# The row-maximum pass of self-attention multiplies 64 rows instead of 128

## Chip, cores and metric

The kernel runs on one core of one Trainium2 chip. The metric is device time in microseconds (us); lower is better.

## What is computed

One transformer block on `x` of shape (2, 1024, 256), with a 77-token context, and behind it a feed-forward layer with quantised weights. In float32:

```
h  = adaln(layernorm(x));  x1 = selfattention(h, h) @ wo + bo + x        # 16 heads of 64, 1024 keys
h2 = adaln(x1);            x2 = crossattention(h2, ctx) @ wo2 + bo2 + x1 # 77 keys
h3 = adaln(x2);            x3 = gated_ff(h3) + x2
out = x + x3 + bitlinear(gelu(bitlinear(layernorm(x + x3))))
scores = q @ k.T / sqrt(64);  attn = softmax(scores)                      # per head
```

Only the self-attention is touched by the change.

## The kernel before

All float32 products are made of float16 pairs: a high part and a low remainder, so that a product `w*x` is three products of float16 (`PASSES`). The work of attention is cut into 16 units of two heads each (`UNITS`; unit `g` holds heads of one batch). The operands of a head lie in `HB` (in the profile `head_operands`), 128 partitions by four fields of 1024 tokens: `QS` holds the high part of the queries in partitions 0 to 63 and the low part in 64 to 127; `KH` holds the high part of the keys in both halves. `QM` and `KL` hold the rest of what the score products need, with the negated row maximum in partition 64 of `QM`. These fields are filled by DMAs from `qk_pairs` (`restack`) and, for the maxima, from `neg_max_rows`.

Self-attention passes over the scores twice. The maximum pass (line 854) makes a 128 by 512 block of scores at a time: 8 tiles of 128 queries by 2 halves of 512 keys, for each of the two heads, so 32 products a unit and 512 in all. VectorE reduces each block to one maximum per query (line 1836, `maxes`), then the two halves to the negated maximum (line 1848), which TensorE transposes into rows (`row`, line 864; for the very first tiles line 867). The second pass makes the scores for the softmax (lines 898 and 899), ScalarE takes the exponential (line 1242), GpSimd or VectorE the float16 remainder (`exps_rest`, line 1568 or 1863), and TensorE multiplies by the values (lines 921 to 923), 48 small products a chunk.

The order on TensorE is written out by hand in `FIRST_UNIT` (unit 0) and `SELF_UNIT` (units 1 to 14); unit 15 takes its order from `unit()`. In it the maximum products of the next heads stand one, or two, at a time between pieces of scores, values, projections (`q`, `k`, `v`, lines 833 and 843; `proj`, line 810) and transposes (`out`, line 871; `norm_T`, line 796):

```
    ("max", 0, 1, 8), ("scores", 1), ("rest", 0), ("max", 0, 1, 9), ("q", 1, 0), ("max", 0, 1, 10), ("slot", 0),
    ("rest", 1), ("scores", 2), ("values", 0), ("rest", 2), ("q", 1, 1), ("scores", 3), ("max", 0, 1, 11),
```

Each maximum product goes to one of two banks of PSUM (`mixed`), and waits until VectorE has read what was in that bank. Setup work of unit 0 ("columns") transposes small arrays of 2 rows (line 765), 16 rows (line 785) and 77 rows (line 789) on TensorE.

Of the kernel before, what the change touches and what calls it, by code (L numbers as in the profile page):

```python
# [22 lines left out]
P = 128  # L23
B, S, D = 2, 1024, 256
CTX = 77
H, DH = 16, 64
# [7 lines left out]
HALF = 512  # L34
# [19 lines left out]
QS, QM, KH, KL = range(4)  # L54
# [354 lines left out]
def build(nc, x, cond, ctx_in, w, out):  # L409
# [6 lines left out]
    with es:  # L416
# [214 lines left out]
        def first_tile(ai, g, what):  # L631

            return TPH if (ai, g, what) == (0, 0, ("row", 0)) else 0
# [114 lines left out]
        def _(pe):  # L748
            mm, tr = nc.tensor.matmul, nc.tensor.transpose
# [3 lines left out]
            for k in range(KC):  # L753
                last = tr(M_[0][:, k * B:(k + 1) * B], condr[:, k * P:(k + 1) * P], identf[0:B, 0:B])
# [59 lines left out]
            def item(ai, g, what, m):  # L814

                a, s, kind = AT[ai], AT[ai].sem, what[0]
                b, hp, par = g // NP, g % NP, g % 2
                wc = [slice(hp * P + c * INNER, hp * P + c * INNER + P) for c in range(KC)]
                if kind in ("q", "k"):
                    if (ai, g) == (0, 0):  # L820
                        pe.wait_ge(hT_done, TPH * (what[1] + 1))
                        pe.wait_ge(split_done, 1 if kind == "q" else 2)
                    elif what == ("q", 0) and hp == 0:
                        pe.wait_ge(hT_done, NT * ai + TPB * (b + 1))
                        pe.wait_ge(split_done, 6 if ai else 2)
                    for n_, (wh, xh) in enumerate(PASSES):
                        for c in range(KC):
                            if kind == "q" or ai == 0:
                                o = b * S + what[1] * HALF
                                rhs = hT[:, xh, c, o:o + HALF]  # L830
                            else:
                                rhs = ctxT[:, xh, c, b, 0:CTX]
                            last = mm(m[:, 0:rhs.shape[-1]], W[:, 0 if kind == "q" else 1, wh, wc[c]], rhs,  # L833
                                      start=(n_ == 0 and c == 0), stop=(n_ == 2 and c == KC - 1))
                elif kind == "v":
                    if g == 0:
                        pe.wait_ge(split_done, 7 if ai else 3)
                    for i in range(a.v_tiles):
                        for n_, (wh, xh) in enumerate(PASSES):
                            for c in range(KC):  # L840
                                o = b * S + (what[1] * a.v_tiles + i) * P
                                lhs = hT[:, xh, c, o:o + P] if ai == 0 else ctxT[:, xh, c, b, 0:CTX]
                                last = mm(m[0:a.ks, i * P:(i + 1) * P], lhs, W[:, 2, wh, wc[c]],  # L843
                                          start=(n_ == 0 and c == 0), stop=(n_ == 2 and c == KC - 1))
                elif kind == "max":

                    _, h, t, kh = what
                    hb = HB[:, par, h, :, :]
                    if (t, kh) == (0, 0):
                        pe.wait_ge(s.heads[h], 16 * a.restack_dmas * (g + 1) + CREDIT)  # L850
                        if (ai, g) == (0, 0):
                            pe.wait_ge(cleared, 16)
                    if ai == 0:
                        last = mm(m[:, :], hb[:, QS, t * P:(t + 1) * P], hb[:, KH, kh * HALF:(kh + 1) * HALF],  # L854
                                  start=True, stop=True)
                    else:
                        for i in range(TPH):
                            q = t * TPH + i
                            last = mm(m[:, i * CTX:(i + 1) * CTX], hb[:, QS, q * P:(q + 1) * P], hb[:, KH, 0:CTX],
                                      start=True, stop=True)  # L860
                elif kind == "row":
                    pe.wait_ge(s.negmax, CREDIT + 2 * g + what[1] + 1)
                    t0 = first_tile(ai, g, what)
                    last = tr(m[0:TPB - t0, 0:P], nm[:, what[1], t0:TPB], identf[:, :])
                elif kind == "first":
                    pe.wait_ge(first_negmax, 1)
                    last = tr(m[0:TPH, 0:P], nm[:, 0, 0:TPH], identf[:, :])
                else:
                    pe.wait_ge(s.summed, CREDIT + 4 * g + 3 + what[1])
                    for i in range(TPH):  # L870
                        last = tr(m[:, i * P:(i + 1) * P], Osb[:, what[1] * TPH + i, :], identf[:, :])
                last.then_inc(s.item, 1)
# [54 lines left out]
            def piece(st):  # L927
                if st.after:
                    pe.wait_ge(*consumed(st.after))
                if st.kind == "item":  # L930
                    item(st.ai, st.g, st.what, ITEM[st.bank])
                elif st.kind == "proj":
                    project(st.ai, *st.what, st.g, st.bank)
                elif st.kind == "normT":
                    norm_T(st.g, st.bank)
                elif st.kind == "scores":
                    scores(st.ai, st.g, st.c)
                elif st.kind == "values":
                    values(st.ai, st.g, st.c)
                elif st.kind == "setup":  # L940
                    setup(st.what)
# [1261 lines left out]
```

## Time and profile before

| | |
|---|---|
| median of 2 runs | 1196.14 us (1196.13 to 1196.16) |
| the profiled execution, first to last instruction | 1200.9 us |
| TensorE (PE) busy | 1115.7 us (93%), 12740 products |
| VectorE (DVE) busy | 860.5 us (72%) |
| GpSimd (POOL) busy | 694.0 us (58%) |
| ScalarE (ACT) busy | 591.5 us (49%) |
| mean granted TensorE clock | 0.990 |

The page gives the profiled execution's span alone, 4.8 us (0.4%) above the median of the timed runs. A product's record on PE outlasts its slot, as products are pipelined, so slots are read from start to start. PEld is the load of the weights (the stationary operand), which has records of its own.

### The profile page before, as it was taken

What the parts mean: (1) busy time and instruction counts of PE and PEld (TensorE: products, weight loads), DVE (VectorE), ACT (ScalarE), POOL (GpSimd) and SP (SyncE); (2) the same over time, 40 slices, a digit from 0 to 9 for tenths busy, and PEclk for the clock granted to TensorE, in tenths of its full rate; (3) what the DMA queues carried; (4) which work ended last, traced back from release to release, by engine and by line L of the source; (5) the groups of instructions that cost most, each with busy time, mean ns of one, the idle gap of its engine ahead of it and who ended that gap; (6) DMA issues with size and microseconds to landing.
All of it is one profiled execution on the core that took longest, in us unless ns stands there. A gap on an engine that the chain in (4) does not pass through costs nothing.

```text
span 1200.9 us, 30653 instructions
## 1 busy us (share of the span) xinstructions
PE 1115.7 (93%) x12740; PEld 731.2 (61%) x12740; DVE 860.5 (72%) x1686; ACT 591.5 (49%) x856; POOL 694.0 (58%) x641
## 2 busy tenths in 40 slices
PE   4799999999999999999999999889899989999996
PEld 1355665665656656657656666567567766756664
DVE  6677767757657568677676576848878976786876
ACT  3445455444444444454443445544444544257677
POOL 5757866765655657777675656346535733533433
PEclk9899999999999999999999999999999989999999
DMA  8330220220220211202202203122433343000001
GB/s 286 86 92 1 55 54 2 55 54 3 54 54 2 55 28 28 55 5 52 54 2 54 54 2 89 41 54 60 136 77 74 72 128 124 1 1 9 15 14 36
DMA packets 41854, 63.52 MB, mean 53 GB/s; under 512 B 11459, under 2 KB 22383, under 8 KB 41461
## 3 DMA queue, kind: packets, MB, share of 16 engines
q1 hardware_dynamic: 40413, 60.91, 20.1%
q8 instruction: 101, 1.65, 0.6%
q10 hardware_dynamic: 1304, 0.66, 0.2%
q14 instruction: 36, 0.29, 0.1%
HBM read 20.63 MB, written 2.10 MB: 19 GB/s over the span
## 4 chain that ended last, share of the span: by engine, by line
PE 67%; DVE 15%; DMA 5%; ACT 5%; issue 4%; POOL 2%; SPq 1%; ACTq 0%; DVEq 0%
PE outs L833 9%; PE scores L898 7%; PE scores L899 7%; PE mixed L854 6%; PE outs L810 5%; PE scores L960 5%; PE outs L923 4%; PE outs L921 4%; DVE maxes L1836 4%; PE outs L922 4%; PE outs L974 4%; PE outs L843 3%; DVE exps_rest L1863 2%; DMA head_operands<-qk_pairs 2%; DMA head_operands<-neg_max_rows 2%
## 5 line engine op out<-in xcount | busy, mean ns | idle before, releaser
L1568 POOL TENSOR_TENSOR exps_rest<-exps 128x1024 f16<-128x1024 f32 (+1 forms) x297 | 510.4, 1723 | 308.3 <-ACT exps L1242 307.2
L1242 ACT ACTIVATE exps<-scores 128x1024 f32<-128x1024 f32 (+1 forms) x320 | 296.8, 937 | 262.9 <-PE scores L899 243.1
L1836 DVE TENSOR_REDUCE maxes<-mixed 128x1 f32<-128x512 f32 x512 | 334.8, 684 | 92.2 <-PE mixed L854 87.7
L921 PE MATMUL outs<-values,exps 128*128 128x65 f16 (+1 forms) x2176 | 227.2, 193 | 1.7 <-POOL exps_rest L1568 1.6
L922 PE MATMUL outs<-values,exps 128*128 128x64 f16 (+1 forms) x2176 | 227.2, 192 | 0.0
L923 PE MATMUL outs<-values,exps_rest 128*128 128x65 f16 (+1 forms) x2176 | 227.0, 194 | 0.0
L898 PE MATMUL scores<-head_operands 128*128 128x512 f16 (+1 forms) x576 | 218.6, 380 | 5.3 <-DMA head_operands<-neg_max_rows 4.7
L899 PE MATMUL scores<-head_operands 128*128 128x512 f16 (+1 forms) x576 | 218.5, 379 | 0.0
L921 PEld LDWEIGHTS outs<-values,exps 128*128 128x128 bf16 (+1 forms) x2176 | 201.9, 98 | 22.3 <-POOL exps_rest L1568 3.1
L922 PEld LDWEIGHTS outs<-values,exps 128*128 128x128 bf16 (+1 forms) x2176 | 200.9, 98 | 23.5
L923 PEld LDWEIGHTS outs<-values,exps_rest 128*128 128x128 f16 (+1 forms) x2176 | 200.8, 97 | 0.0
L854 PE MATMUL mixed<-head_operands 128*128 128x512 f16 x512 | 178.0, 384 | 18.2 <-DVE maxes L1836 9.8
L833 PE MATMUL outs<-hT,weights 128*128 128x512 f16 x492 | 123.8, 389 | 3.4 <-DVE qk_pairs L1821 2.4
L1821 DVE SCALAR_TENSOR_TENSOR qk_pairs<-outs,qk_pairs 128x512 f16<-128x512 f32 x82 | 56.4, 688 | 80.5 <-ACT qk_pairs L1207 80.5
L854 PEld LDWEIGHTS mixed<-head_operands 128*128 128x128 f16 x512 | 48.7, 97 | 78.0 <-DVE maxes L1836 34.7
L810 PE MATMUL outs<-weights,attn_outT 128*128 128x256 f16 x744 | 93.0, 276 | 0.0
L899 PEld LDWEIGHTS scores<-head_operands 128*128 128x128 f16 (+1 forms) x576 | 57.6, 100 | 48.9
L960 PE MATMUL scores<-hT,weights 128*128 128x512 f16 x384 | 86.8, 379 | 0.0
L898 PEld LDWEIGHTS scores<-head_operands 128*128 128x128 f16 (+1 forms) x576 | 57.5, 100 | 47.8 <-issue 7.2
L1207 ACT ACTIVATE qk_pairs<-outs 128x512 f16<-128x512 f32 x82 | 49.0, 597 | 71.3 <-PE outs L833 70.3
L833 PEld LDWEIGHTS outs<-hT,weights 128*128 128x128 f16 x492 | 44.6, 100 | 57.0 <-DVE attn_outT L1856 7.8
L810 PEld LDWEIGHTS outs<-weights,attn_outT 128*128 128x128 f16 x744 | 72.0, 99 | 11.6
(204 smaller groups left out, 1597.6 us busy)
## 6 DMA issues: line engine op xcount, KB each, us to landing
head_operands<-qk_pairs SPq DMA_DIRECT2D x128, 256.0 KB, 3.9
head_operands<-qk_pairs SPq DMA_DIRECT2D x32, 128.0 KB, 2.5
stage<-in_L_xcond_ff_w_dram SPq DMA_DIRECT2D x3, 1024.0 KB, 5.0
residual<-in_x_dram SPq DMA_DIRECT2D x4, 512.0 KB, 9.8
stage<-in_L_ffn_w_dram SPq DMA_DIRECT2D x2, 1024.0 KB, 5.1
head_operands<-in_x_dram SPq DMA_DIRECT2D x1, 2048.0 KB, 9.5
out_dram<-out_tile SPq DMA_DIRECT2D x16, 128.0 KB, 1.7
attn_outT<-in_L_xcond_attn_wq_dram SPq DMA_DIRECT2D x1, 1024.0 KB, 8.4
```

Source lines behind the costliest of these rows:

```text
L810: last = mm(ITEM[bank][:, 0:D], OT[:, c, xh, t * P:(t + 1) * P], W[:, 3, wh, c * D:(c + 1) * D], start=(n_ == 0 and c == 4 * half), stop=( ...
L833: last = mm(m[:, 0:rhs.shape[-1]], W[:, 0 if kind == "q" else 1, wh, wc[c]], rhs, start=(n_ == 0 and c == 0), stop=(n_ == 2 and c == KC - 1))
L854: last = mm(m[:, :], hb[:, QS, t * P:(t + 1) * P], hb[:, KH, kh * HALF:(kh + 1) * HALF], start=True, stop=True)
L898: mm(o, kb[:, KH, :], hb[:, QS, :], start=True, stop=False)
L899: last = mm(o, kb[:, KL, :], hb[:, QM, :], start=False, stop=True)
L921: mm(o, eb[:, sl], vb[:, DH:VW], start=(kt == 0 and q == 0), stop=False, skip_group_check=True)
L922: mm(o[:, 0:DH], eb[:, sl], vb[:, 0:DH], start=False, stop=False, skip_group_check=True)
L923: last = mm(o, R[0:a.ks, slot, sl], vb[:, DH:VW], start=False, stop=(kt == a.kt - 1), skip_group_check=True)
L960: last = mm(SP_[f % 2][:, half * HALF:(half + 1) * HALF], WU[:, wh, k, half * F + f * P:half * F + (f + 1) * P], hT[:, xh, k, tc * HALF:(t ...
L1242: A(E[0:a.ks, c % RING, 0:n], SP_[c % 2][0:a.ks, 0:n], ACT.Exp, scale=SCALE).then_inc(s.exps, 1)
L1568: G.tensor_tensor(R[0:a.ks, c % RING, 0:n], e, e.bitcast(BF16).rearrange("p (n two) -> p n two", two=2)[:, :, 1], ALU.subtract).then_inc(s ...
L1836: V.tensor_reduce(mx[:, h, t, kh:kh + 1], m[:, :], AX_X, ALU.max).then_inc(s.maxed, 1)
```

## The change

The product of the maximum pass takes partitions 0 to 63 of both operands alone. Before, it summed (query high + query low) times key high over 128 rows; now it is query high times key high over 64 rows, which the compiler places in the 64-row form of the array. Instruction counts, their order, the columns streamed (512), the columns of the weights (128), all waits and all buffers stay as they are. The scores of the second pass keep all their terms.

```diff
@@ -851,7 +851,7 @@
                         if (ai, g) == (0, 0):
                             pe.wait_ge(cleared, 16)
                     if ai == 0:
-                        last = mm(m[:, :], hb[:, QS, t * P:(t + 1) * P], hb[:, KH, kh * HALF:(kh + 1) * HALF],
+                        last = mm(m[:, :], hb[0:DH, QS, t * P:(t + 1) * P], hb[0:DH, KH, kh * HALF:(kh + 1) * HALF],
                                   start=True, stop=True)
```

## Rows read from the trace of the kernel before

**Rows 1.** The page: busy time, then the span in 40 slices, then the last chain.
```profile
PE 1115.7 (93%) x12740; PEld 731.2 (61%) x12740; DVE 860.5 (72%) x1686; ACT 591.5 (49%) x856; POOL 694.0 (58%) x641
...
PEclk9899999999999999999999999999999989999999
...
PE 67%; DVE 15%; DMA 5%; ACT 5%; issue 4%; POOL 2%; SPq 1%; ACTq 0%; DVEq 0%
```

**Rows 2.** Windows around the maximum pass: busy us (x instructions) of each engine, clock.
```profile
44.00:58.00 14.00, 12.10 (x80) 6.49 (x81) 11.65 (x23) 3.51 (x6) 11.87 (x14) 0.68 0.25 59
58.00:777.00 719.00, 687.21 (x8878) 443.74 (x8876) 504.22 (x881) 341.67 (x426) 465.81 (x279) 1.00 0.17 40
```

**Rows 3.** Groups of PE and PEld by line and form, whole run.
```profile
L854 PE MATMUL mixed<-head_operands 128*128 128x512 f16 x512 | 178.0, 384 | 18.2 <-DVE maxes L1836 9.8 <-issue 4.1 <-DMA head_operands<-qk_pairs 3.8
...
L854 PEld LDWEIGHTS mixed<-head_operands 128*128 128x128 f16 x512 | 48.7, 97 | 78.0 <-DVE maxes L1836 34.7 <-issue 9.4
```

**Rows 4.** Timeline of PE, 301 to 302.5 us: start, us, line, operation.
```profile
301.26 0.81 PE L833 MATMUL outs<-hT,weights 128*128 128x512 f16 x3
301.91 0.59 PE L854 MATMUL mixed<-head_operands 128*128 128x512 f16 x2
302.34 0.19 PE L921 MATMUL outs<-values,exps 128*128 128x65 f16 x1
302.37 0.20 PE L922 MATMUL outs<-values,exps 128*128 128x64 f16 x1
302.40 0.19 PE L923 MATMUL outs<-values,exps_rest 128*128 128x65 f16 x1
```

**Rows 5.** Timeline of PE: the first and the last maximum product.
```profile
44.49 0.58 PE L854 MATMUL mixed<-head_operands 128*128 128x512 f16 x1 [4.06 <-issue]
...
776.69 0.38 PE L854 MATMUL mixed<-head_operands 128*128 128x512 f16 x1
```

**Rows 6.** Timeline of PE in cross-attention, 850 us: value products of 77 rows.
```profile
850.27 0.20 PE L921 MATMUL scores<-values,exps 77*128 77x65 f16 x1
850.30 0.19 PE L922 MATMUL scores<-values,exps 77*128 77x64 f16 x1
850.33 0.19 PE L923 MATMUL scores<-values,exps_rest 77*128 77x65 f16 x1
```

**Rows 7.** Timelines of PE and PEld, 53 to 55.3 us: from 128 rows to 2.
```profile
53.37 1.50 PE L843 MATMUL outs<-weights,hT 128*128 128x128 f16 x24
54.65 0.22 PE L843 MATMUL outs<-weights,hT 128*128 128x128 f16 x1
54.80 0.22 PE L765 MATMUL scores<-identf,exps_rest 2*128 2x2 f32 x1
54.80 0.13 PEld L765 LDWEIGHTS scores<-identf,exps_rest 2*128 2x128 f32 x1
54.95 0.38 PE L765 MATMUL scores<-identf,exps_rest 2*128 2x2 f32 x4
55.26 0.20 PE L765 MATMUL scores<-identf,exps_rest 2*128 2x2 f32 x1
```

**Rows 8.** Timelines of PE and PEld, 55.3 to 55.7 us: from 16 rows to 77.
```profile
55.32 0.21 PE L785 MATMUL scores<-identf,exps 16*128 16x16 f32 x1
55.46 0.29 PE L789 MATMUL scores<-identf,stage 77*128 77x77 f32 x1
55.46 0.14 PEld L789 LDWEIGHTS scores<-identf,stage 77*128 77x128 f32 x1
```

**Rows 9.** Timelines of PEld and PE: neighbours of other shapes and types.
```profile
52.99 0.22 PE L843 MATMUL outs<-weights,hT 128*128 128x128 f16 x1
53.04 0.27 PE L867 MATMUL mixed<-identf,neg_max 128*4 128x128 f32 x1
52.99 0.09 PEld L867 LDWEIGHTS mixed<-identf,neg_max 128*4 128x4 f32 x1
53.05 0.10 PEld L854 LDWEIGHTS mixed<-head_operands 128*128 128x128 f16 x1
55.72 0.23 PE L789 MATMUL scores<-identf,stage 77*128 77x77 f32 x1
55.72 0.10 PEld L854 LDWEIGHTS mixed<-head_operands 128*128 128x128 f16 x1
```

**Rows 10.** Who waited for whom on PE, 58 to 777 us: total, times, longest.
```profile
PE mixed L854 <- DVE maxes L1836: 8.8, 20, 1.2
PE mixed L864 <- DVE neg_max L1848: 8.5, 11, 1.7
PE outs L871 <- DVE attn_out L1876: 5.7, 15, 0.4
PE mixed L854 <- DMA head_operands<-qk_pairs: 3.8, 4, 1.1
PE scores L898 <- DMA head_operands<-neg_max_rows: 1.4, 2, 1.1
PE outs L833 <- DVE qk_pairs L1821: 0.7, 1, 0.7
PE outs L921 <- POOL exps_rest L1568: 0.5, 1, 0.5
```

## Prediction

> **What bounds the kernel now.** I read the page first [rows 1]: TensorE is busy 93% of the span, VectorE 72%, the others less than 60%, and the last chain runs through PE for 67%. The granted clock is at full speed, 2.4 GHz, in nearly every slice. Then the windows [rows 2]: between 58 and 777 us, where 500 of the 512 maximum products lie, PE has 687.2 us of records in 719.0 us at clock 1.00, while VectorE has 504, GpSimd 466 and ScalarE 342. So this stage is bound by TensorE, and whatever lengthens the slots of its products comes out at the end, less what it takes from PE's own waits. From 44 to 58 us the clock is 0.68 and VectorE sets the pace (11.65 of 14 us); that stretch is short. After 777 us nothing of the changed line runs.
>
> The third view is the groups by line [rows 3]: 512 products of 128 rows by 512 columns. Their records of 384 ns are pipelined; the slot is read from start to start [rows 4]: two products from 301.91, the next line at 302.34, so 0.216 us each, the time of 512 columns at 2.4 GHz. In all they hold 512 x 0.216 = 110.6 us of PE. The value products beside them follow each other every 0.03 us. Nothing is lost where one line hands over to another: the load of the next weights begins while the product before it streams.
>
> The fourth view is TensorE's rows in order of time, from the first maximum product to the last [rows 5]. I counted along them how the 512 stand: 224 alone, 138 in pairs, one run of 3 and one of 9, which makes 364 runs. Each has work of 128 (or 77) rows before and behind it. So the change makes the array go from its full form to the 64-row form 364 times and back 364 times: **728 changes of form**, where this stage had two.
>
> **Part one: the product itself.** It streams the same 512 columns and loads the same 128 columns of weights, from 64 rows. The nearest rows for fewer rows are the value products of cross-attention, 77 rows [rows 6], which start every 0.03 us, as those of 128 rows do [rows 4]. I cost the shorter contraction at nothing, gain or loss. The bounds: a gain of half a slot is a rival below; a loss in the load is bounded by 0.03 us, the rate at which such loads follow each other in the value products, and 138 inner products of pairs could pay it, 4 us.
>
> The Trainium skill, "TensorEngine Tiling (Array Packing)", section Theoretical Speedup, promises up to 2x for a contraction of 64 or less. By the same page that comes from separate tiles working side by side, and here one product is issued at a time into one tile; no run here shows two at once. If it held for a lone product, it would be the first rival below.
>
> **Part two: the changes of form.** The trace of before has two places where TensorE goes between products of very few rows and of many. Going in [rows 7]: 24 products of line 843 start from 53.37 on, the last at 54.65, one every 0.056 us. The first 2-row transpose of line 765 starts at 54.80, 0.15 later, and its weight load starts at 54.80 too. The load did not run ahead; it started 0.15 us after the product in front, whose columns take 0.053, so it came 0.095 after the last column. That is 0.094 lost, and the first record is 0.22 long against 0.20 for its later sisters, another 0.02 for the load that is not hidden. Coming out [rows 8]: the 16-row transpose starts at 55.32, the first 77-row one at 55.46, 0.14 later, again with its load at the same moment; the slot of such small transposes is 0.062 (five of them from 54.95 to 55.26 [rows 7]), so 0.08 lost, and its record is 0.29 long where a later sister has 0.23 [rows 9], 0.06 more for a float32 load. So the two changes cost 0.116 and 0.14 us.
>
> Is it the number of rows, and not type, shape or a new line, that does it? In [rows 9] a float32 transpose with 4 weight columns follows a float16 product after 0.05, and its load starts at 52.99, together with the product before it. And from the last 77-row float32 transpose (55.72) to the 128-row maximum product the load starts at 55.72 as well. From 128 to 77 rows, float32 to float16 and 128 to 4 columns, all hand over without a gap; 128 to 2 and 16 to 77 do not. So the gap belongs to the form of the array. That 64 rows are a form apart from 128 is my inference, from the description of the change and from 77 being no form apart; no row of before has 64 rows.
>
> The rule for this stands in the Trainium skill, "TensorEngine Tiling (Array Packing)", section Key Properties: changing the tiling mode drains the engine. The trace agrees at both places. The skill's "TensorE: Matmul & The Clock Gate", section Single matmul latency, has a fixed part of about 166 ns in a lone warm product; as an estimate from that page, 728 x 0.166 = 121 us would be added if the whole of it were exposed at each change. The rows say 0.116 and 0.14, and they decide.
>
> For the change at hand I take the drain of 0.095 after the last column, and 0.03 for an exposed float16 load (the rate of loads in the value products [rows 4], less than the 0.06 of float32). That is 0.125 us per change, and it is the same going in and out, as the drain counts from the end of the stream and not from its length. 728 x 0.125 = **91 us**. Bounds per change: 0.116 from below (84 us in all); from above the time by which a maximum product's record outlasts its slot, 0.38 - 0.216 = 0.164, plus the load of 0.03, 0.194 (141 us in all).
>
> **Part three: what the waits of PE take back.** In a wait, the array has drained already, and later arrival at a wait shortens it. PE waits 54 times in the stage, 29.4 us in all [rows 10], nearly all for VectorE, which waits on TensorE itself and is slowed less than it. At least one change per wait is absorbed, 54 x 0.125 = 7 us; at most all the time without a PE record, 719.0 - 687.2 = 32 us [rows 2]. I take two changes per wait, one at the wait and one between it and the wait before, 54 x 0.25 = 13 us: nearer to the low end, since the waits bunch up around `neg_max` and the last maxima, and a wait for VectorE often starts from a TensorE product that is itself late. No new wait comes in: the same semaphores are waited on in the same order. The DMAs, GpSimd and ScalarE have more time than before, and need none. What is next late is still TensorE.
>
> **Sum.** 91 - 13 = 78 us more. Against the profiled span this is 1200.9 + 78 = 1279; against the median of the runs, which is 4.8 us less, 1196.1 + 78 = **1274 us**, 6.5% slower. With the bounds: 84 - 32 = 52 gives 1248; 141 - 7 = 134 gives 1330.
>
> **Rivals.**
> First, faster: a product of 64 rows holds the array for half its time. Place: each of the 512 slots; price 0.108 us each, 55 us, so 1141 us if changes of form were free. It decides only from the point where a change of form costs less than 55 / 728 = 0.076 us. For it speaks nothing in the trace; against it, 77 rows go at the pace of 128 [rows 4, 6]. Chance 0.04.
>
> Second, no change: 64 rows hand over as 77 do. Either the 64-row form isn't used, or the gaps at 54.7 and 55.4 us come from the very small forms alone, or from a wait the records do not name (the first transpose of line 765 has one for data that was ready long before). Then the time stays 1196, perhaps a few us off. Against it: two gaps with the same signature, the second with no wait at all. Chance 0.12.
>
> Third, only one direction pays, say the way into the small form, while the way out is hidden because the full form's load can run ahead. 364 x 0.125 - 13 = 32 us, so 1228. Against it: [rows 8] show the way out and its load not ahead. Chance 0.06.
>
> Fourth, the drain is longer behind a product of 512 columns than behind the short ones seen, up to the whole tail of the record: 141 - 13 = 128 us, so 1324. Chance 0.05.
>
> The forecast has the rest, 0.73. A measurement of this kernel can tell about 2% from no change, 24 us. Slower by more: forecast, third and fourth, 0.84; I give 0.83, as a third case could end just inside. Within 2%: 0.13. Faster: 0.04. For the range I leave out the first two rivals (0.16) and the end of the fourth: 1228 to 1312.
>
> **What the changed profile would show.** Line 854 has form 64*128, still 512 of them, with a slot of 0.216 inside a pair. The product behind a run starts some 0.34 us after the last of the run, not 0.216, and its weight load starts with it instead of one slot earlier; likewise into a run: behind a value product the maximum product comes some 0.155 later instead of 0.03. PE's share of busy time hardly moves, as the tails of the records cover most of each gap, but the stretch from first to last maximum product grows from 732 to about 810 us, while after it nothing changes. The granted clock stays 1.00. Waits for `maxes` and `neg_max` shrink from 17 us to less than 10.
>
> **What would make it wrong.** That the load starts a slot ahead at the seams of the two forms would overturn part two. A granted clock that falls in the stage would add far more than any of this: at half clock each slot of 0.216 becomes 0.43; the trace held 1.00 here through waits of up to 1.7 us [rows 2, 10], and gaps of 0.1 us are smaller. And if PE's waits soak up much more than 13 us, the sum is too high by the difference, 19 us at most.

## The result and the profile after

The changed kernel takes 1247.7 us (median of 2 runs, 1246.7 to 1248.7), 1.0408 times before, with an interval of 1.0369 to 1.0447. The forecast was 1274 us, range 1228 to 1312: slower, as forecast, by 51.6 us instead of 78. The profiled execution has a span of 1244.9 us, 44.0 more than that of before.

The page of the changed kernel: busy time, and the chain that ended last. The granted clock stays at 0.99 over the run.

```profile
PE 1176.6 (95%) x12733; PEld 712.3 (57%) x12740; DVE 861.2 (69%) x1686; ACT 591.7 (48%) x856; POOL 694.2 (56%) x641
...
PE 83%; DVE 9%; issue 3%; ACT 3%; DMA 2%; SPq 0%; POOL 0%; ACTq 0%; DVEq 0%
```

PE's part of the last chain went from 67% [rows 1] to 83%; the other engines do the same work in a longer run. The windows of the same stretches as [rows 2], the second now ending at 825:

```profile
44.00:58.00 14.00, 12.22 (x73) 6.94 (x74) 9.56 (x16) 2.61 (x4) 12.11 (x14) 0.55 0.23 54
58.00:825.00 767.00, 749.70 (x8880) 425.09 (x8880) 507.17 (x887) 343.03 (x427) 466.20 (x279) 1.00 0.16 38
825.00:1245.00 420.00, 392.11 (x3729) 272.89 (x3732) 320.90 (x719) 226.19 (x399) 191.05 (x293) 0.99 0.23 58
```

The clock of the stage is 1.00 as before. The time without a PE record fell from 719.0 - 687.2 = 31.8 to 767.0 - 749.7 = 17.3 us. The first and the last maximum product in the timeline, against [rows 5]:

```profile
44.78 0.58 PE L854 MATMUL mixed<-head_operands 64*128 64x512 f16 x1 [4.10 <-issue]
...
825.09 0.39 PE L854 MATMUL mixed<-head_operands 64*128 64x512 f16 x1
```

The stage between them takes 780.3 us, where it took 732.2: 48.1 more. What comes behind took 1200.9 - 776.7 = 424.2 and takes 1244.9 - 825.1 = 419.8. So the loss is in the stage of the maximum pass, and the 4 us less behind it touch nothing that was changed: the clock after 777 us was 0.98 in the execution of before, and is 0.99 here. Timed runs of before vary by as much (1195.9 to 1205.9 in the experiments below).

```profile
777.00:1201.00 424.00, 393.82 (x3730) 273.56 (x3727) 321.05 (x718) 226.19 (x398) 191.41 (x293) 0.98 0.23 57
```

Some 2 of the 48 us arise before 58 us, and most of that belongs to the clock and not to the changes of form: the granted clock goes from 0.50 (1.2 GHz) to full speed near 53 us in the execution of before and near 57 us in this one (0.68 and 0.55 between 44 and 58), and the 11th maximum product comes 13.2 us after the first instead of 11.3. In the experiments below the clock rises between 49 and 54 us with 128 or 65 rows and between 50 and 57 us with 64 or 32, so whether the change delays it is not shown.

Now the seams themselves. The timelines of PE and PEld around 304 us of the changed kernel; the last number in brackets is idle time before the instruction:

```profile
303.76 0.38 PE L899 MATMUL scores<-head_operands 128*128 128x512 f16 x1
304.07 0.39 PE L854 MATMUL mixed<-head_operands 64*128 64x512 f16 x1
304.39 0.20 PE L921 MATMUL outs<-values,exps 128*128 128x65 f16 x1
304.43 0.20 PE L922 MATMUL outs<-values,exps 128*128 128x64 f16 x1
...
304.06 0.09 PEld L854 LDWEIGHTS mixed<-head_operands 64*128 64x128 f16 x1 [0.42 <-DVE maxes L1836]
304.38 0.10 PEld L921 LDWEIGHTS outs<-values,exps 128*128 128x128 bf16 x1 [0.23 <-issue]
304.40 0.10 PEld L922 LDWEIGHTS outs<-values,exps 128*128 128x128 bf16 x1
```

The score product starts at 303.76 and the maximum product 0.31 later, not 0.216; its load starts at 304.06, right with it, instead of one slot earlier. On the way out it is the same: 304.07 to 304.39 is 0.32, with the load at 304.38. I read all of them between 58 and 825 us in this way. The 361 ways in lose 0.096 us each (median; eight in ten lie between 0.095 and 0.097), behind a product of 512 columns and behind one of 65 alike; the 362 ways out lose 0.102 or 0.092 (medians of the two kinds), the smaller where the last product of the run was its second. In a pair, line 854 of this timeline has:

```profile
320.50 0.60 PE L854 MATMUL mixed<-head_operands 64*128 64x512 f16 x2
321.03 0.20 PE L921 MATMUL outs<-values,exps 128*128 128x65 f16 x1
```

320.50 to 321.03 for two slots and a way out, 0.53: 0.226 for the first product, 0.216 + 0.092 for the second. So the product just behind a change has a slot longer by 0.010, in either form (the first score product behind a run too), and the others keep 0.216. Each change costs 0.099 on average, 728 x 0.099 = 72 us, and the 0.010 that is not in these numbers (the first product of a pair, and the product just behind a run) adds some 3: **75 us on TensorE, of which 48 arrive.** Where the product behind a run is a float32 transpose of 128 columns, its slot is 0.164 (median of 34) instead of 0.110, about 1 us more in all. Who waited for whom on PE between 58 and 825 us:

```profile
PE mixed L864 <- DVE neg_max L1848: 8.4, 11, 1.4
PE outs L871 <- DVE attn_out L1876: 4.4, 15, 0.3
PE mixed L854 <- DVE maxes L1836: 2.2, 7, 0.6
PE scores L898 <- DMA head_operands<-neg_max_rows: 1.1, 1, 1.1
PE mixed L854 <- DMA head_operands<-qk_pairs: 0.8, 1, 0.8
PE outs L833 <- DVE qk_pairs L1821: 0.4, 1, 0.4
```

54 waits of 29.4 us [rows 10] became 36 of 17.3, most of the difference at the banks of `mixed` (8.8 to 2.2). This view counts only what is left behind the record of the product in front, and that record outlasts the slot by 0.163, so it hides a part. From start to start, minus the slot and minus 0.1 at a change, PE lost 50 us to waits in the stage before (134 waits of over 0.04 us) and 23 to 25 after (69 waits). So waits gave back some 25 us, and 75 - 25 is about the 48 measured.

### The profile page after: what moved, and what is told of

The parts are those of the page before. It is cut to its first block, busy times and chain, and to the rows that moved or that the text cites. A ratio compares the mean times of both kernels' runs of the same rounds, so it can differ in the third digit from the quotient of the medians.

```text
span 1244.9 us, 30646 instructions
## 1 busy us (share of the span) xinstructions
PE 1176.6 (95%) x12733; PEld 712.3 (57%) x12740; DVE 861.2 (69%) x1686; ACT 591.7 (48%) x856; POOL 694.2 (56%) x641
## 4 chain that ended last, share of the span: by engine, by line
PE 83%; DVE 9%; issue 3%; ACT 3%; DMA 2%; SPq 0%; POOL 0%; ACTq 0%; DVEq 0%
PE mixed L854 11%; PE scores L898 10%; PE scores L899 9%; PE outs L833 9%; PE outs L921 6%; PE outs L810 6%; PE outs L923 5%; PE outs L922 5%; PE scores L960 5%; PE outs L843 4%; PE outs L974 3%; PE outs L871 2%; DVE maxes L1836 2%; PE scores L833 2%; DMA head_operands<-neg_max_rows 1%
## 5 line engine op out<-in xcount | busy, mean ns | idle before, releaser
L854 PE MATMUL mixed<-head_operands 64*128 64x512 f16 x512 | 177.1, 388 | 8.1 <-issue 4.1
L854 PEld LDWEIGHTS mixed<-head_operands 64*128 64x128 f16 x512 | 39.1, 93 | 115.7 <-DVE maxes L1836 55.1
```

Source lines behind the costliest of these rows:

```text
L854: last = mm(m[:, :], hb[0:DH, QS, t * P:(t + 1) * P], hb[0:DH, KH, kh * HALF:(kh + 1) * HALF], start=True, stop=True)
```

## The experiments

Each ran in three rounds beside the kernel before, on one chip with the others of its group; times are medians. The kernel before had 1199.6, 1200.0, 1200.2 and 1198.7 us in the four groups.

### 65 and 32 rows: is it the form of the array?

```diff
-  hb[0:DH, QS, ...], hb[0:DH, KH, ...]
+  hb[0:DH + 1, QS, ...], hb[0:DH + 1, KH, ...]     # 65 rows
+  hb[0:32, QS, ...], hb[0:32, KH, ...]             # 32 rows
```

> The maximum product takes 65 rows (the 64 high parts and one row of the low parts; the other 63 low rows are left out of the maxima). Theory A, changes of the array's form cost: 65 rows lie in the full form as the 77 rows of cross-attention do, there are no changes of form, so the time is that of before, 1196 us, within 4 us. Rival B, a product over fewer rows is itself slower beside products over 128: about 1245 us, as with 64 rows.

> The maximum product takes 32 rows (half of the high parts; the rest is left out of the maxima). Theory A: another small form, entered and left at the same 728 places, each with a drain of the same length, so 1248 us, within 6 us. Rival: the drain shrinks with the rows of the form it leaves; leaving 32 rows would then cost less than leaving 64, and the time would be 1225 to 1240 us.

65 rows: 1201.0 us, ratio 1.001 (0.9983 to 1.0037). One row more than in the changed kernel, and the whole loss is gone. Its timeline of PE:

```profile
300.60 0.60 PE L854 MATMUL mixed<-head_operands 65*128 65x512 f16 x2
301.04 0.19 PE L921 MATMUL outs<-values,exps 128*128 128x65 f16 x1
```

Two products in 0.44 us and no gap behind them. It is not quite nothing: the first product of 65 rows in a run has a slot of 0.220 instead of 0.216, and the full product behind a run 0.003 more than before, between 2 and 3 us in all, which the times cannot tell from zero. 32 rows: 1248.3 us, ratio 1.0419 (1.040 to 1.0439), the same as 64. A way in and a way out in its timeline:

```profile
76.68 0.38 PE L899 MATMUL scores<-head_operands 128*128 128x512 f16 x1
76.99 0.38 PE L854 MATMUL mixed<-head_operands 32*128 32x512 f16 x1
77.31 0.39 PE L898 MATMUL scores<-head_operands 128*128 128x512 f16 x1
```

0.31 in and 0.32 out, as with 64 rows. So 64 rows are a form apart from 65 and more, and the drain is the same with 32 rows as with 64. That fewer rows are slower by themselves (rival of the first), and that the drain shrinks with them (rival of the second), both fell.

### The same products in fewer runs: is it the changes, or the products?

The written orders of units 0 to 14 are passed through a function that holds each first maximum product back until the second comes, so that 512 products stand in 255 runs instead of 364.

```diff
+def pair_up(order):
+    out, held = [], None
+    for entry in order:
+        if entry[0] != "max":
+            out.append(entry)
+        elif held is None:
+            held = entry
+        else:
+            out += [held, entry]
+            held = None
+    return tuple(out)
+FIRST_UNIT, SELF_UNIT = pair_up(FIRST_UNIT), pair_up(SELF_UNIT)
```

> The written order of units 0 to 14 is changed so that the maximum products stand in pairs (the first of two moves down to the second); 128 rows as before. The control for the next kernel. There are no changes of form in it; pairs need both banks free at once, so a few more waits for VectorE: 1196 to 1206 us.

> The same order in pairs, 64 rows: still 512 products of 64 rows, but 255 runs of them instead of 364, so 510 changes of form instead of 728. Theory A, 0.102 us a change less what the waits take back: 510 x 0.102 = 52, less 25, 27 us over the pairs with 128 rows (20 to 35). Rival B, the cost is per product of 64 rows: 51 us over the pairs with 128 rows, as in the order of before.

With 128 rows this order takes 1219.1 us, ratio 1.0157 (1.0136 to 1.0178): worse than expected, since pairs wait longer for VectorE. Who waited, between 58 and 800 us:

```profile
PE mixed L880 <- DVE neg_max L1864: 16.3, 26, 2.3
PE mixed L870 <- DVE maxes L1852: 12.9, 47, 0.8
```

(16.3 and 12.9 against 8.5 and 8.8 us [rows 10]; the inserted lines shift the numbers by 16. From start to start, all waits are 67 us instead of 50.) With 64 rows it takes 1247.5 us. The step from 128 to 64 rows is 28.4 us in this order and 51.6 (44 to 53 by the interval) in the order of before. 512 products of 64 rows are in both; what differs is 510 changes of form against 728. Rival B, a price for each product, asked for 51 and fell; 27 was expected of the changes. The number of waits differs between the orders as well, so the closeness of 28 to 27 is not a measurement of 0.1 us; the timelines are. In them the 64-row kernel has some 52 us at its changes and 43 us of waits instead of 67: 52 - 24 is the 28 measured.

### One head: who pays first?

```diff
+  n_rows = DH if h == 0 else P
+  last = mm(m[:, :], hb[0:n_rows, QS, ...], hb[0:n_rows, KH, ...], ...)
```

> Only the first head of each unit uses 64 rows, the second keeps 128: 256 products and 364 to 370 of the 728 changes of form. Changes at 0.102 us each: 37 us. Theory A1, the waits of TensorE take back their share first: 37 less 13 to 25 us, 1208 to 1220 us, less than half of the 51 us that both heads cost. Rival, the waits take back in proportion or the cost is per product: 1221 us.

1226.3 us, ratio 1.0248 (1.0218 to 1.0279), 27 us more than before, outside the 1208 to 1220 of theory A1, and above the rival's 1221 too. Its trace has 345 changes of form, not the 364 to 370 expected, so 47% of the changes cost half of the loss or a little more: from start to start, waits gave back only 8 of some 35 us here, as against 25 of 75. Theory A1, that waits pay first, fell. The reason I see, argued and not shown: a wait takes back only what is lost between it and the work that its releaser waited for, so the waits among the second head's products, with no change in front of them, stayed.

### Was it the waits that took 25 us back?

First attempt: make VectorE's reduction of a block shorter, so that TensorE waits less from the start.

```diff
-  V.tensor_reduce(mx[:, h, t, kh:kh + 1], m[:, :], AX_X, ALU.max)
+  V.tensor_reduce(mx[:, h, t, kh:kh + 1], m[:, 0:HALF // 2], AX_X, ALU.max)
```

> The kernel before, but VectorE's reduction of each block reads 256 of its 512 columns (the other half is left out of the maxima). TensorE's waits for VectorE, up to 50 us from start to start, shrink: 1165 to 1185 us. It is the base for the next kernel.

> The same shorter reduction with 64 rows. Theory A: the seams of the forms cost 74 us on TensorE whatever the rest does, and in the changed kernel waits for VectorE took back 25 of them; with those waits gone beforehand the difference to the kernel with the short reduction and 128 rows rises to 60 to 74 us. Rival: the seams cost only the 50 us seen, and the waits have no part in it; then the difference stays 46 to 52 us.

1186.7 us with 128 rows and 1239.4 with 64: a step of 52.6 us. That lies at the edge of the rival's range and below that of theory A, but the base did not do what it was made for. It gained only 13 us, and most of its waits stayed: by start to start 36 us instead of 50, of which the 64-row kernel kept 15. The transposes of the attention output, behind VectorE's line 1876, now wait as long as the maximum products:

```profile
PE outs L871 <- DVE attn_out L1876: 5.9, 15, 0.4
PE mixed L854 <- DVE maxes L1836: 5.8, 17, 1.0
```

By its starts the pair fits the account (75 less the 21 that waits gave back), but its time does not tell the two theories apart. Second attempt: fill the waits with work. Each maximum product is issued twice into its bank, in both kernels. The changes of form stay 728.

```diff
+  for _ in range(2):
+      last = mm(m[:, :], hb[0:DH, QS, ...], hb[0:DH, KH, ...], start=True, stop=True)   # 0:P in the base
```

> The kernel before, with each maximum product issued twice into its bank (128 rows). It adds 512 x 0.216 = 110.6 us of TensorE work at the same places, so that hardly any of TensorE's 50 us of waits for others is left: 1196 + 110 - 25 to 40 = 1266 to 1281 us. It is the base for the next kernel.

> Each maximum product issued twice, 64 rows; 364 runs and 728 changes of form as in the changed kernel. Theory A, the changes cost 76 us on TensorE and waits gave 25 of it back: with the waits of the base filled beforehand the difference to the kernel with 128 rows is 65 to 80 us. Rival: the changes cost only the 50 us that the time showed; the difference stays 46 to 54 us. If the product of 64 rows were slower by itself, 512 more of them would add: over 100 us.

1273.2 us with 128 rows, 1345.7 with 64: a step of **72.5 us**, where the order and the number of changes are those of the changed kernel. The windows of the stage, first the base, then 64 rows (each from its own trace):

```profile
58.00:851.00 793.00, 783.76 (x9374) 492.39 (x9373) 508.79 (x881) 342.13 (x426) 466.91 (x280) 1.00 0.16 37
```

```profile
58.00:924.00 866.00, 858.58 (x9410) 454.92 (x9408) 511.70 (x890) 343.97 (x429) 467.94 (x280) 1.00 0.14 34
```

Time without a PE record is 9.2 us in the base (31.8 in the kernel before) and 7.4 in the other. From start to start the base has 17 us of waits left and the other 12, so 5 us or little more could be given back where the changed kernel gave back 25, and the changes cost nearly what the timelines add up to, 75 us. The 512 further products of 64 rows add nothing of their own: a price for each product would have made over 100. A run of four in the timeline of the 64-row kernel:

```profile
300.11 1.03 PE L855 MATMUL mixed<-head_operands 64*128 64x512 f16 x4
301.07 0.20 PE L922 MATMUL outs<-values,exps 128*128 128x65 f16 x1
```

That is 0.96 for four slots (0.864), the longer first slot (0.010) and one way out (0.092). This shows both halves of the account: 75 us of seams, of which waits take back some 25 in the changed kernel and little where the waits are filled beforehand.

### Two row tiles side by side: is there something that the form can give?

```diff
+  r0 = kh * DH
+  last = mm(m[:, :], hb[r0:r0 + DH, QS, ...], hb[r0:r0 + DH, KH, ...], ...)
```

> 64 rows for every maximum product, but the second half of the keys takes rows 64 to 127 (query low parts times key high parts; its high parts are left out of the maxima), so that the two products of a pair go into two row tiles of the same form. Theory A: the changes of form stay 728 and a change of tile inside the form drains nothing, so at least no slower than 1248 us. If two tiles work side by side, the second product of a pair starts well before 0.216 us after the first, and up to 138 x 0.2 = 28 us come back: 1220 us. If a change of row tile drains as well: 138 x 0.1 = 14 us more, 1262 us.

1231.1 us, ratio 1.0284 (1.0255 to 1.0314): 17 us better than the changed kernel, and than 32 rows beside it, but not the 28 that were possible, and still slower than before. A pair in its timeline:

```profile
317.66 0.39 PE L855 MATMUL mixed<-head_operands 64*128 64x512 f16 x2
317.98 0.20 PE L922 MATMUL outs<-values,exps 128*128 128x65 f16 x1
```

Two products in one record of 0.39, and the next line 0.32 after the first: the second starts 0.004 us behind the first (median of 138 pairs; in 29 of them it comes late, behind a wait for its bank), so a pair that meets takes the time of one. A change of tile inside the form drains nothing. The same in the order of pairs:

> The order in pairs, with the second half of the keys in rows 64 to 127 (its high parts are left out of the maxima): 247 pairs side by side and some 510 changes of form. Against the pairs of 64 rows in one tile (1247.5 us) each pair saves the slot of its second product, 247 x 0.222 = 55 us, 1193 us, if nothing else waits. With the same share kept as in the order of before (17 of 30 us, since both banks come full at once and VectorE needs 1.4 us to empty them), 31 us: 1216 us. Rival: VectorE takes nearly all of it back, 1235 to 1245 us.

1234.5 us, ratio 1.0277 (1.0241 to 1.0313): 13 us better than the same order with one tile (which ran in another group, with nearly the same time before, 1200.0 and 1200.2), at the end of the rival's range, not the 31 or 55 of the expectation. Its timeline has a pair that does not meet and one that does:

```profile
300.36 0.39 PE L871 MATMUL mixed<-head_operands 64*128 64x512 f16 x1
300.96 0.39 PE L871 MATMUL mixed<-head_operands 64*128 64x512 f16 x1 [0.21 <-DVE maxes L1853]
301.60 0.63 PE L888 MATMUL outs<-identf,attn_out 128*128 128x128 f32 x4 [0.25 <-DVE attn_out L1893]
...
303.02 0.39 PE L871 MATMUL mixed<-head_operands 64*128 64x512 f16 x2
```

At 300.96 the second product waits for its bank, and the two do not meet. That is so in 63 of 248 pairs; 182 start within 0.02 us. The larger loss is that all waits, from start to start, grow from 43 us with one tile to 80. There are two banks, and VectorE empties one in 0.69 us, as a row of the kernel with two tiles in the order of before shows (its line 1837):

```profile
310.06 0.69 DVE L1837 TENSOR_REDUCE maxes<-mixed 128x1 f32<-128x512 f32 x1 [2.02 <-PE mixed L855]
```

So neither use of two tiles is faster than the kernel before: a pair side by side takes 0.216 + 0.2 for its two changes, against 0.432 for two products of 128 rows, and the waits take the rest. By that sum it would need longer runs, and with them more banks; those were not tried, as the other banks of this kernel hold scores and outputs.

## Why the prediction was right, and where its size was off

- **What bounds the kernel** held: TensorE, in the stage of the maximum pass, which grew by 48 us while the rest did not grow.
- **The product itself at nothing** held. A slot is 0.216 inside the form, and 65, 64 and 32 rows stream alike to within 0.004. The bound of 4 us for loads in pairs was 1.4 (138 x 0.010).
- **728 changes of form, read from two places with few rows** held: the signature (the load no longer ahead) is that of [rows 7] and [rows 8], and the inference that 64 is a form apart is shown by 65 against 64. The sentence of "TensorEngine Tiling (Array Packing)" in the Trainium skill, section Key Properties, that changing the mode drains the engine, agrees with 723 changes read here, at 0.092 to 0.102 us. The estimate from "TensorE: Matmul & The Clock Gate" in the Trainium skill, section Single matmul latency, 121 us from a fixed part of 166 ns, is too much by over half.
- **The first term was mis-sized**: 728 x 0.125 = 91 us; measured 75, which is also below the 84 us given as the lower bound. That bound was taken from 0.116 at a float32 transpose, and the float16 changes here cost 0.103. The drain of 0.095 was right (the load starts 0.307 behind a product that streams 0.213, 0.094). Wrong was the 0.03 added for the exposed load. I took the rate at which such loads follow each other; the records show the product starting 0.004 behind its load and its own slot longer by 0.010. In float16 the exposed part is 0.01. Behind a run, the float32 transposes of 128 columns pay 0.054 (0.164 instead of 0.110), which fits the 0.06 read as a longer float32 load at the way out of before; the 0.02 at the way in stays unexplained.
- **The second term was mis-sized too**: 13 us taken back; measured about 25, inside the bounds of 7 and 32. I counted the 54 waits that the waits view shows; by starts there were more of them, 134 over 0.04 us, hidden behind the tails of the records. The 16 us of the first term and the 12 of this one are 28, about the 26 between 78 and the 52 of the timed runs (30 to the 48 of the profiled stage). Both terms missed to the same side, so nothing cancelled: by the bounds of the prediction's own sum the time was to be 1248 to 1330 us, and 1247.7 lies at their very end; the stated range reached further down for the sake of the third rival, and that it holds the result with room to spare is luck.
- **Rivals.** Faster by halved slots: fell for one product at a time; true only for two tiles at once. No change: fell. Only one direction pays: 1228 us was 20 off, and both directions are seen. Longer drain behind 512 columns: it is 0.096 behind 512 columns and behind 65.
- **Signs named ahead**: form 64*128, slot 0.216, load with the product, clock 1.00, all seen. The way out was put at 0.34 and is 0.32; the way in from a value product at 0.155 and is 0.12 to 0.13. The stage at about 810 us is 780. Not foreseen was that the clock would rise later before 58 us, which is most of 2 us. Waits for `maxes` and `neg_max` were to fall from 17 to under 10 us and stand at 10.6.

## What to carry to other kernels

Count the places where TensorE goes between products of at most 64 rows and of more, not the products: each passage costs 0.1 us here, and that is a half slot of 512 columns. A product of 64 rows by itself is no faster than one of 128 (0.216 both), so a small form can gain only with tiles side by side, and pairs of them did not yet pay here. Where a contraction of 64 stands between full ones, 65 rows keep the full form at a cost too small to show in the time (1201.0 against 1199.6 us). And price the waits of the bound engine by starts rather than by idle behind records; half of them were given back here, and only a kernel with most of its waits filled showed nearly the full price.

## What the runs showed that was not expected

- The drain is 0.095 us whatever the form left or entered has (32, 64 or 128 rows) and whatever streams in front (65 or 512 columns).
- The product just behind a change has a slot of 0.226 instead of 0.216, in either form; with 65 rows in place of 64, which is no change of form, there is still 0.003 to 0.004.
- Two products in row tiles 0 to 63 and 64 to 127 start 0.004 us apart when both banks are free, and take one slot together.
- Putting 512 products in pairs, with nothing else changed, costs 19 us here: waits from start to start rise from 50 to 67 us, with two banks and a reader that needs 0.69 us for each.
